# A new order for the opening of the second layer: batch 0's keys and key pieces before all queries, batch 0's probabilities inside the first substitution

## Chip, cores and metric

The kernel runs on one core of a Trainium2 chip. The metric is the device time of one execution in microseconds (us), as the median of several runs; lower is better. The engines are PE (TensorE matmuls, with PEld for its weight loads), DVE (VectorE), ACT (ScalarE), POOL (GpSimd) and SP, which issues most of the transfers.

## What is computed

Two transformer-like layers over `x` (4 batches, 256 tokens, 256 channels). Each layer has a gated recurrent branch, an attention and a feed-forward part (ternary weights in the first, eight experts with capacity in the second). The edit touches the attention of the second layer, whose values are first corrected by a triangular solve:

```python
q, k = _rope(q, k)
s = jnp.einsum('bihd,bjhd->bhij', k, k) * scale
s = jnp.where(strict, s, -jnp.inf)
m = jnp.max(s, axis=-1, keepdims=True)
e = jnp.exp(s - m)                      # 0 where not strict
p = e / denom
L = p * beta[..., None]
A = L + jnp.eye(T)
u = jax.scipy.linalg.solve_triangular(A, v, lower=True)
sc = jnp.where(causal, jnp.einsum('bihd,bjhd->bhij', q, k) * scale, -jnp.inf)
o = jnp.einsum('bhij,bhjd->bihd', softmax(sc), u) @ Wo
```

## The kernel before

The work is a list of steps, `ORDER`, that `make_order` (from line 253) writes out by hand. Every engine runs through this list and issues, for each step, the part that is its own; so the list sets the order on PE, ACT, POOL and SP. For DVE the function `lag` moves some steps a little later. Semaphores order the engines against one another; within one engine nothing overtakes.

For batch b of the second layer the steps are these.

- `requant` b (DVE L1806 to L1810) adds the quantized feed-forward output of the first layer to `x`; `gate` 2 b (ACT tanh L1329, DVE L1634) makes the layer's input.
- `proj` 1 b 1 projects the keys, `proj` 1 b 0 the queries: PE, then the rotation on DVE (L1652 to L1655). `split` cuts the result into three bfloat16 parts on DVE (L1664 to L1672). SP stores the parts to memory (L816) and loads them again in another layout, the stacks (L804): behind a key split eight loads (stack `k` and stack `kq`), behind a query split none; the four loads of stack `q` are the step `qload`. There are three `k` stacks, two `kq` and two `q`. The parts of keys, and those of queries, have one buffer each, so a split waits until the last store of its kind has landed.
- `kscores` (nine pieces): keys against keys on PE, the row maxima on DVE (L1687 to L1695), exponentials with their sums on ACT (L1408). `kmax` turns the maxima on PE (L1033) and copies them on ACT (L1364), and SP puts them as rows below the stack `kq` (L852). `kdiag` then gives the diagonal blocks transposed (PE, ACT L1385), `den` and `blocks` scale them (DVE L1825 to L1836), and POOL inverts all 32x32 blocks of the batch in a chain of small operations (L2077 to L2086). `kprobs` (eight pieces) gives the blocks below the diagonal (PE, ACT L1392).
- `inverse` b: DVE moves POOL's result out (L1845). POOL starts the next batch's blocks only behind that. Then eight rounds of `solve` (PE, DVE copy L1867, SP copies L866) and `update` (PE L1138, DVE L1853 and L1856): the substitution.
- `vproj` projects the values (PE, ACT L1354, DVE L1819). `scores` (twelve pieces, DVE maxima L1705), `minus` and `max`, `probs` (twelve pieces, ACT L1373) and `pv` are the attention with the solved values.

Most steps that write to PSUM take one of four banks in turn, the ring `mid`; PE waits until the step four places earlier in that ring has been read.

The steps of later batches are put between the rounds of the substitution by `spread`: `ahead[b]` is the list of what is done during batch b's. In the kernel before, all keys and queries of batches 0 and 1 come first, then the key pieces; the `probs` of batch 0 and the `vproj` of batch 2 stand right ahead of `inverse` 0, and the first substitution holds batch 2's key pieces, batch 3's keys, queries and values, and batch 1's scores.

Of the kernel before, what the change touches and what calls it, by code (L numbers as in the profile page):

```python
# [38 lines left out]
B, T, D = 4, 256, 256  # L39
# [26 lines left out]
NK = 3  # L66
# [188 lines left out]
def make_order():  # L255
    def groups(kind, layer, b):
        n = {"kscores": KG, "kprobs": KP}.get(kind, NGS[layer])
        return [(kind, layer, b, j) for j in range(n)]


    o = first_layer()[0]

    def vproj(b):
        return [("vproj", b, 0), ("vproj", b, 1)]
# [4 lines left out]
    def otr(b):  # L269
        return [[("otr", 1, b, 0)], [("otr", 1, b, 1)]]  # L270

    def keys_then_queries(b):
        return [("proj", 1, b, 1), ("split", 1, b, 1), ("proj", 1, b, 0), ("split", 1, b, 0)]

    o += [("requant", 0), ("gate", 2, 0)] + keys_then_queries(0) + [("qload", 0)] + vproj(0) + [("requant", 1), ("gate", 2, 1)]
    o += keys_then_queries(1) + [("qload", 1)] + vproj(1) + [("requant", 2), ("requant", 3), ("gate", 2, 2)]
    o += groups("kscores", 1, 0) + [("kmax", 1, 0)] + groups("scores", 1, 0)[:6] + [("kdiag", 0, 0), ("kdiag", 0, 1), ("den", 0), ("blocks", 0)]
    o += groups("kprobs", 1, 0) + groups("scores", 1, 0)[6:] + [("minus", 1, 0), ("max", 1, 0)]
    o += groups("kscores", 1, 1) + [("kmax", 1, 1)] + keys_then_queries(2)
    o += [("kdiag", 1, 0), ("kdiag", 1, 1), ("den", 1), ("blocks", 1)] + groups("kprobs", 1, 1) + groups("probs", 1, 0) + [("qload", 2)] + vproj(2)  # L280

    def one_each(steps):
        return [[step] for step in steps]

    def queries(b):
        return one_each(groups("scores", 1, b)) + [[("minus", 1, b), ("max", 1, b)]]

    def out(b):
        return [[("oT", 1, b)], [("wo", 1, b), ("gate", 3, b)]]

    p1, p2, p3 = (one_each(groups("probs", 1, b)) for b in range(1, B))
    def inverted(b):
        return one_each(groups("kscores", 1, b)) + [[("kmax", 1, b)]], [[("kdiag", b, 0)], [("kdiag", b, 1), ("den", b), ("blocks", b)]]

    (k2, d2), (k3, d3) = inverted(2), inverted(3)
    ahead = [k2 + [[("gate", 2, 3)], [("proj", 1, 3, 1), ("split", 1, 3, 1)]] + d2 + [[("proj", 1, 3, 0), ("split", 1, 3, 0)]] + one_each(vproj(3))
             + queries(1),
             k3 + otr(0) + d3 + p1[:4] + [[("oT", 1, 0)]] + p1[4:8] + out(0)[1:] + p1[8:] + [[("qload", 3)]] + queries(2),
             otr(1) + p2[:4] + [[("oT", 1, 1)]] + p2[4:8] + out(1)[1:] + p2[8:]
             + queries(3),  # L300
             otr(2) + p3[:4] + [[("oT", 1, 2)]] + p3[4:8] + out(2)[1:] + p3[8:]]
    for b in range(B):

# [25 lines left out]


ORDER = make_order()


# [97 lines left out]
def program(nc, d):  # L431

    with ExitStack() as ctx:
# [69 lines left out]
        oT = v3(take(CT * T), CT)  # L503
# [180 lines left out]
        ones_ready = sem("ones_rows_ready")  # L684
# [13 lines left out]
        parts_ready = [sem(f"{n}_parts_ready") for n in ("q", "k")]  # L698
# [196 lines left out]
        def _(pe):  # L895
# [14 lines left out]
            for step in ORDER:  # L910
                kind = step[0]
                i = count.get(kind, 0)
                count[kind] = i + 1
                if kind == "proj":
                    layer, b = step[1:3]
# [6 lines left out]
                    for o in step[3:] or (0, 1):  # L922
                        out = bank_of(slot) if layer else big(slot, o)
# [11 lines left out]
                elif kind == "vproj":  # L935

                    _, b, a = step
# [35 lines left out]
                elif kind == "kdiag":  # L973

                    _, b, a = step
                    pe.wait_ge(mrows["kq", b % 2], row_count("kq", 1, b))
                    if b == 0:
                        pe.wait_ge(ones_ready, NK)
                    slot = acquire(step)
                    q_, k_ = stack["kq", b % 2], stack["k", stack_of("k", 1, b)]  # L980
                    mask = maskb[:, KQ_STRICT, :]
# [1034 lines left out]
        def _(pool):  # L2016
# [19 lines left out]
            for step in ORDER:  # L2036
# [14 lines left out]
                elif kind == "quant":  # L2051
                    pool.wait_ge(amax_in, 1)
                    G_.partition_all_reduce(small[:, 65:66], small[:, 64:65], P, RED.max).then_inc(amax_out, 1)
                    pool.wait_ge(amax_out, 1)
                elif kind == "qload" and step[1] == 0:
                    pool.wait_ge(parts_ready[0], B + 1)
                    wait_done(pool, ("fc2", B - 1), "act")
                    pool.wait_ge(gate_ready, NUMBER["weigh", 3, B - 1] + 1)
                    ones_rows(2)
# [120 lines left out]
```

## Time and profile before

| | us |
|---|---|
| median of 3 runs (lowest, highest) | 781.09 (777.92, 781.1) |
| the profiled execution | 783.57 |
| its span in the trace | 781.8 |
| first layer | about 0 to 314 |
| POOL inverts batch 0's blocks | 377.43 to 420.61 |
| DVE moves the inverses of batches 0 to 3 | 424.88, 484.74, 549.45, 593.35 |

The span is the time from the first instruction of the trace to the last; the profiled execution's own time also holds what lies around it. A timeline row gives start and duration, the engine, the line of the kernel, the operation with its operands, a count, and in brackets how long the engine had been idle and what released it. Consecutive equal instructions are merged into one row with the start of the first and the time to the end of the last.

### The profile page before, as it was taken

Reading aid. Unit: us, or ns where it says so; the run is one execution under the profiler, and the core shown is the slowest. Engines: PE = TensorE matmul, PEld = TensorE weight load, DVE = VectorE, ACT = ScalarE, POOL = GpSimd, SP = SyncE. Lnnn points to the kernel's source line nnn. Section 1 sums busy time; section 2 is a strip of 40 time slices with the busy share of each in tenths; the row PEclk is TensorE's granted clock in tenths of the full one; section 3 lists DMA queues with packets and bytes.
Section 4 is the critical chain, followed back from the end, with each engine's and each line's share of the span. In section 5 each row is a group of like instructions: output and inputs, shape, how many; then the busy total and the mean of one; then the engine's idle time right before and its main releaser. Section 6 shows DMA issues by size and latency. Waiting matters only on the chain.

```text
span 781.8 us, 17527 instructions
## 1 busy us (share of the span) xinstructions
PE 512.3 (66%) x7117; PEld 416.5 (53%) x7117; DVE 566.9 (73%) x1184; ACT 329.5 (42%) x779; POOL 214.1 (27%) x313
## 2 busy tenths in 40 slices
PE   0451754895595853444647577758887873799995
PEld 0341643784485742332435355536654653799995
DVE  6899599797859994678676877666475446768861
ACT  4335243453355622006365611433411343368771
POOL 3000000000000000000685881880683001325443
PEclk9965656896798977665667676659898856699999
DMA  8055005032000020175007133002202238256622
GB/s 310 22 118 122 0 18 105 1 85 38 1 2 1 1 55 0 49 156 122 4 3 158 13 75 61 7 5 49 64 10 63 31 143 283 88 153 204 191 29 27
DMA packets 48209, 56.02 MB, mean 72 GB/s; under 512 B 25136, under 2 KB 42048, under 8 KB 43648
## 3 DMA queue, kind: packets, MB, share of 16 engines
q1 hardware_dynamic: 44784, 49.90, 24.7%
q0 software_dynamic: 3344, 4.99, 3.4%
q8 instruction: 56, 0.92, 0.5%
q14 instruction: 25, 0.20, 0.1%
HBM read 43.15 MB, written 10.49 MB: 69 GB/s over the span
## 4 chain that ended last, share of the span: by engine, by line
PE 37%; DVE 27%; issue 8%; ACT 4%; DMA 1%; POOL 1%; SPq 0%; POOLq 0%; DVEq 0%; ACTq 0%
PE psum L904 32%; DVE arena L1705 3%; PE psum L1138 3%; DVE arena L1687 2%; DVE arena L1856 2%; ACT psum L1408 1%; DVE arena L1692 1%; DVE arena L1695 1%; DVE arena L1693 1%; DVE arena L1853 1%; DVE arena L1590 1%; DVE arena L1618 1%; DVE arena L1634 1%; DVE psum L1654 1%; DVE arena L1655 1%
## 5 line engine op out<-in xcount | busy, mean ns | idle before, releaser
L904 PE MATMUL psum<-arena 32*32 32x16 f32 (+20 forms) x5281 | 354.6, 278 | 192.1 <-DVE arena L1634 76.6
L904 PEld LDWEIGHTS psum<-arena 98*32 98x32 bf16 (+8 forms) x5281 | 273.6, 128 | 269.7 <-DVE arena L1634 79.3
L2086 POOL TENSOR_TENSOR arena<-arena 128x31 f32<-128x31 f32 (+15 forms) x124 | 69.0, 556 | 9.7
L1705 DVE TENSOR_REDUCE arena<-psum 128x4 f32<-128x1024 f32 (+2 forms) x80 | 59.7, 789 | 11.6 <-PE psum L904 11.1
L1373 ACT ACTIVATE arena<-psum 128x512 f32<-128x512 f32 (+1 forms) x80 | 50.5, 687 | 40.0 <-PE psum L904 40.0
L2084 POOL TENSOR_TENSOR arena<-arena 128x31 f32<-128x31 f32 (+15 forms) x124 | 64.4, 520 | 9.7
L1408 ACT ACTIVATE psum<-psum,arena 128x256 f32<-128x256 f32 (+7 forms) x128 | 45.3, 367 | 27.8 <-DVE arena L1695 27.5
L1604 DVE TENSOR_TENSOR_SCAN arena<-arena 128x255 f32<-128x255 f32 x64 | 42.5, 727 | 11.4 <-ACT arena L1318 11.3
L2065 POOL DMA_DIRECT2D arena<-wq x1 | 0.9, 862 | 171.9 <-PE psum L904 171.9
L1318 ACT ACTIVATE arena<-arena 128x255 f32<-128x255 f32 x64 | 27.2, 498 | 46.4 <-DVE arena L1590 46.4
L2110 POOL DMA_INDIRECT out<-arena x16 | 31.2, 1948 | 48.9 <-DVE arena L2010 46.8
L2100 POOL DMA_INDIRECT arena<-dispatched,arena x16 | 19.6, 1227 | 84.7 <-DVE arena L1977 81.0
L1992 DVE TENSOR_TENSOR fc_second_parts<-arena,fc_first_parts 128x2048 fp32r<-128x2048 f32 x16 | 36.6, 2290 | 7.8 <-ACT fc_first_parts L1515 7.7
L904 PE MATMUL psum<-input_first_parts,fc_first_parts 128*128 128x256 f32 x128 | 39.0, 305 | 1.3 <-DVE input_second_parts L1986 1.3
L1487 ACT ACTIVATE psum<-psum,arena 128x256 f32<-128x256 f32 x64 | 24.6, 448 | 35.7 <-PE psum L904 35.7
L1138 PE MATMUL psum<-arena 32*32 32x224 f32 (+6 forms) x896 | 36.2, 307 | 5.0 <-DVE arena L1867 3.0
L1590 DVE TENSOR_TENSOR_SCAN arena<-arena 128x256 f32<-128x256 f32 x64 | 39.0, 672 | 0.5
L904 PE MATMUL psum<-fc_first_parts,hidden_first_parts 128*128 128x256 f32 x128 | 36.8, 288 | 2.5 <-DVE hidden_second_parts L2003 2.5
L904 PE MATMUL psum<-input_second_parts,fc_first_parts 128*128 128x256 f32 x128 | 38.2, 299 | 0.0
L904 PE MATMUL psum<-input_first_parts,fc_second_parts 128*128 128x256 f32 x128 | 38.2, 298 | 0.0
L904 PE MATMUL psum<-fc_first_parts,hidden_second_parts 128*128 128x256 f32 x128 | 36.2, 283 | 0.0
L904 PE MATMUL psum<-fc_second_parts,hidden_first_parts 128*128 128x256 f32 x128 | 36.2, 283 | 0.0
(185 smaller groups left out, 890.4 us busy)
## 6 DMA issues: line engine op xcount, KB each, us to landing
arena<-fc SPq DMA_DIRECT2D x16, 1024.0 KB, 5.0
arena<-parts SPq DMA_DIRECT2D x40, 256.0 KB, 4.6
parts<-arena SPq DMA_DIRECT2D x16, 384.0 KB, 3.6
arena<-parts SPq DMA_DIRECT2D x40, 128.0 KB, 5.5
arena<-arena SPq DMA_DIRECT2D x128, 8.0 KB
arena<-xT SPq DMA_DIRECT2D x1, 1024.0 KB, 10.4
arena<-w1T SPq DMA_DIRECT2D x1, 1024.0 KB, 10.8
arena<-w2T SPq DMA_DIRECT2D x1, 1024.0 KB, 13.0
```

Source lines behind the costliest of these rows:

```text
L904: return nc.tensor.matmul(out, lhsT, rhs, start=start, stop=stop)
L1138: last = nc.tensor.matmul(acc(half)[rows, qq, (s + 1) * BLK:T], ublk[rows, s, q, :], later[b % 2][s][rows, q, :], start=s == 0 and qq == 0 ...
L1318: A(scan[s + 1][:, ct, 0:T - 1], scan[s][:, ct, 0:T - 1], ACT.Copy, scale=back[:, i:i + 1]).then_inc(scaled, 1)
L1373: ins = A(prob[:, first:end, 0:T] if early else prob[:, first:end, T:T + P], src, ACT.Exp, scale=scale)
L1408: ins = A(s_, s_, ACT.Exp, bias=nbias[:, n:n + 1], accum_out=ncc[b][:, n:n + 1])
L1590: ins = V.tensor_tensor_scan(scan[s][:, ct, :], dd, src[:, ct, bt(b)], 0.0, ALU.mult, ALU.add)
L1604: st(V.tensor_tensor_scan(scan[s][:, ct, T - 2::-1], dd, scan[s + 1][:, ct, T - 2::-1], scan[s][:, ct, T - 1:T], ALU.mult, ALU.add))
L1705: ins = V.tensor_reduce(mneg[:, at + first:at + end], src, axis=AX.X, op=ALU.max, negate=True)
L1992: V.tensor_tensor(second[:], fcw[e % NW][i], first[:].bitcast(F32), ALU.subtract).then_inc(w_second[i], 1)
L2084: link(G_.tensor_tensor(tmp, A3[:, k + 1:BLK, k:k + 1].to_broadcast([P, rows, w]), X3[:, k:k + 1, 0:w].to_broadcast([P, rows, w]), ALU.mult))
L2086: ins = G_.tensor_tensor(X3[:, k + 1:BLK, 0:w], X3[:, k + 1:BLK, 0:w], tmp, ALU.add)
L2110: G_.indirect_dma_start(out=d["out"], out_offset=bass.IndirectOffsetOnAxis(ap=ids[:, 2 * e + s:2 * e + s + 1], axis=0), in_=eo[e % 2][:, s ...
```

## The change

Only the order changes, with two waits that follow from it.

- Keys and queries are separate steps now. Batch 0's keys and its `vproj` come first, then the remaining three `requant`, the second `gate`, and batch 0's key pieces at once. Batch 1's keys follow, then the inverse's blocks of batch 0, and only then the queries of batches 0 and 1.
- Batch 1's key pieces stand behind that; batch 0's scores and batch 1's blocks behind those; batch 2's keys last.
- Batch 2's queries and `vproj` and batch 0's `probs` move into the first substitution. The `probs` alternate with batch 2's key pieces; batch 2's queries stand right ahead of batch 3's.
- POOL clears the third stack's rows of ones and the padding of the solution behind batch 0's key split instead of behind its `qload`. The `kdiag` of batches 0 and 2 wait for the rows of ones of their own stack.

```diff
-    def keys_then_queries(b):
-        return [("proj", 1, b, 1), ("split", 1, b, 1), ("proj", 1, b, 0), ("split", 1, b, 0)]
-
-    o += [("requant", 0), ("gate", 2, 0)] + keys_then_queries(0) + [("qload", 0)] + vproj(0) + [("requant", 1), ("gate", 2, 1)]
-    o += keys_then_queries(1) + [("qload", 1)] + vproj(1) + [("requant", 2), ("requant", 3), ("gate", 2, 2)]
-    o += groups("kscores", 1, 0) + [("kmax", 1, 0)] + groups("scores", 1, 0)[:6] + [("kdiag", 0, 0), ("kdiag", 0, 1), ("den", 0), ("blocks", 0)]
-    o += groups("kprobs", 1, 0) + groups("scores", 1, 0)[6:] + [("minus", 1, 0), ("max", 1, 0)]
-    o += groups("kscores", 1, 1) + [("kmax", 1, 1)] + keys_then_queries(2)
-    o += [("kdiag", 1, 0), ("kdiag", 1, 1), ("den", 1), ("blocks", 1)] + groups("kprobs", 1, 1) + groups("probs", 1, 0) + [("qload", 2)] + vproj(2)
+    def keys(b):
+        return [("proj", 1, b, 1), ("split", 1, b, 1)]
+
+    def queries_of(b):
+        return [("proj", 1, b, 0), ("split", 1, b, 0)]
+
+    o += [("requant", 0), ("gate", 2, 0)] + keys(0) + vproj(0) + [("requant", 1), ("requant", 2), ("requant", 3), ("gate", 2, 1)]
+    o += groups("kscores", 1, 0) + [("kmax", 1, 0)] + keys(1) + [("kdiag", 0, 0), ("kdiag", 0, 1), ("den", 0), ("blocks", 0)]
+    o += queries_of(0) + [("qload", 0)] + groups("kprobs", 1, 0) + queries_of(1) + [("qload", 1)] + vproj(1)
+    o += groups("kscores", 1, 1) + [("kmax", 1, 1), ("gate", 2, 2)] + groups("scores", 1, 0)[:6]
+    o += [("kdiag", 1, 0), ("kdiag", 1, 1), ("den", 1), ("blocks", 1)] + groups("scores", 1, 0)[6:] + [("minus", 1, 0), ("max", 1, 0)]
+    o += keys(2) + groups("kprobs", 1, 1)
...
-    ahead = [k2 + [[("gate", 2, 3)], [("proj", 1, 3, 1), ("split", 1, 3, 1)]] + d2 + [[("proj", 1, 3, 0), ("split", 1, 3, 0)]] + one_each(vproj(3))
-             + queries(1),
+    p0 = one_each(groups("probs", 1, 0))
+    mixed = [unit for pair in zip(k2, p0) for unit in pair] + p0[len(k2):]
+    ahead = [mixed + one_each(vproj(2)) + [[("gate", 2, 3)], keys(3)] + d2 + [queries_of(2), [("qload", 2)], queries_of(3)]
+             + one_each(vproj(3)) + queries(1),
...
-                    if b == 0:
-                        pe.wait_ge(ones_ready, NK)
+                    if b in (0, NK - 1):
+                        pe.wait_ge(ones_ready, b + 1)
...
-                elif kind == "qload" and step[1] == 0:
-                    pool.wait_ge(parts_ready[0], B + 1)
+                elif step == ("split", 1, 0, 1):
+                    pool.wait_ge(parts_ready[1], B + 1)
```

The lines of the changed kernel are four higher behind the edit (L1687 is L1691 there, and so on).

The first place is on DVE, behind the last key piece of batch 0. Before, batch 0's scores (L1705) followed, then `den` and `blocks`:

```order
L1687 TENSOR_REDUCE arena<-psum 128x4
L1692 TENSOR_SCALAR arena<-arena 128x4
L1693 SCALAR_TENSOR_TENSOR arena<-arena 128x4
L1695 TENSOR_TENSOR arena<-arena 128x4
L1705 TENSOR_REDUCE arena<-psum 128x2 x2
L1705 TENSOR_REDUCE arena<-psum 128x4
L1705 TENSOR_REDUCE arena<-psum 128x2 x2
L1705 TENSOR_REDUCE arena<-psum 128x4
L1825 TENSOR_SCALAR arena<-arena 128x32
```

Now the rotation (L1656 to L1659) and the split (L1668 to L1676) of batch 1's keys follow, then `den`:

```order
L1691 TENSOR_REDUCE arena<-psum 128x4
L1696 TENSOR_SCALAR arena<-arena 128x4
L1697 SCALAR_TENSOR_TENSOR arena<-arena 128x4
L1699 TENSOR_TENSOR arena<-arena 128x4
L1656 TENSOR_TENSOR arena<-psum,arena 128x512
L1658 TENSOR_TENSOR psum<-psum,arena 128x512
L1659 TENSOR_TENSOR arena<-arena,psum 128x512
L1668 CAST arena<-arena 128x512
L1673 TENSOR_TENSOR arena<-arena 128x512
L1674 CAST arena<-arena 128x512
L1676 TENSOR_TENSOR arena<-arena 128x512
L1829 TENSOR_SCALAR arena<-arena 128x32
```

What followed DVE's own pieces were scores, whose matmuls PE could do ahead; now it is a projection that PE issues behind `kmax`.

The second place is on DVE around the move of batch 0's inverse (L1845, now L1849), which the first `solve` copy and the first key piece of batch 2 follow. Before, `blocks` of batch 1 and the `vproj` of batch 2 (L1819) stood ahead of it, and batch 2's keys had been split earlier:

```order
L1836 STREAM_TRANSPOSE arena<-arena 128x1024
L1819 TENSOR_TENSOR arena<-psum,arena 128x16 x2
L1845 STREAM_TRANSPOSE arena<-arena 128x32x32
L1867 COPY arena<-psum 128x2x16 x2
L1687 TENSOR_REDUCE arena<-psum 128x2
```

Now the rotation and split of batch 2's keys stand right ahead of it:

```order
L1656 TENSOR_TENSOR arena<-psum,arena 128x512
L1658 TENSOR_TENSOR psum<-psum,arena 128x512
L1659 TENSOR_TENSOR arena<-arena,psum 128x512
L1668 CAST arena<-arena 128x512
L1673 TENSOR_TENSOR arena<-arena 128x512
L1674 CAST arena<-arena 128x512
L1676 TENSOR_TENSOR arena<-arena 128x512
L1849 STREAM_TRANSPOSE arena<-arena 128x32x32
L1871 COPY arena<-psum 128x2x16 x2
L1691 TENSOR_REDUCE arena<-psum 128x2
```

Between the split of batch 2's keys and the first piece that uses them, DVE now has the move and one `solve` copy.

The third place is on SP, in the first substitution from batch 3's key store on. L816 stores parts, L804 loads stacks, L866 copies the solution. Before, one query store stood behind the eight loads:

```order
L816 DMA parts<-arena 128x6x256
L804 DMA arena<-parts 32x4096 x2
L804 DMA arena<-parts 16x4096 x3
L804 DMA arena<-parts 32x4096 x2
L804 DMA arena<-parts 16x4096
L866 DMA arena<-arena 32x4x16 x4
L816 DMA parts<-arena 128x6x256
L866 DMA arena<-arena 32x4x16 x16
```

Now batch 2's query store and its four loads come behind the key loads, and batch 3's query store behind them (the lines are L820, L808 and L870):

```order
L820 DMA parts<-arena 128x6x256
L808 DMA arena<-parts 32x4096 x2
L808 DMA arena<-parts 16x4096 x3
L808 DMA arena<-parts 32x4096 x2
L808 DMA arena<-parts 16x4096
L820 DMA parts<-arena 128x6x256
L808 DMA arena<-parts 16x4096
L808 DMA arena<-parts 32x4096 x2
L808 DMA arena<-parts 16x4096
L870 DMA arena<-arena 32x4x16 x4
L820 DMA parts<-arena 128x6x256
L870 DMA arena<-arena 32x4x16 x8
```

Two query stores, with a set of loads between them, stand where one stood.

## Rows read from the trace of the kernel before

**Rows 1.** The page: the span, and each engine's busy time.
```profile
span 781.8 us, 17527 instructions
PE 512.3 (66%) x7117; PEld 416.5 (53%) x7117; DVE 566.9 (73%) x1184; ACT 329.5 (42%) x779; POOL 214.1 (27%) x313
```
**Rows 2.** Timeline of POOL: batch 0's inverse starts and ends, batch 1's starts.
```profile
377.43 1.91 POOL L2077 TENSOR_TENSOR arena<-arena 128x1024 f32<-128x1024 f32 x1 [43.48 <-DVEq L1838]
...
420.36 0.25 POOL L2086 TENSOR_TENSOR arena<-arena 128x31 f32<-128x31 f32 x1
426.96 1.91 POOL L2077 TENSOR_TENSOR arena<-arena 128x1024 f32<-128x1024 f32 x1 [6.35 <-DVE arena L1845]
```
**Rows 3.** Timeline of DVE: batch 2's vproj, and the moves of the four inverses.
```profile
424.67 0.17 DVE L1819 TENSOR_TENSOR arena<-psum,arena 128x16 f32<-128x16 f32 x1 [0.77 <-ACT arena L1354]
424.88 1.91 DVE L1845 STREAM_TRANSPOSE arena<-arena 128x1024 f32<-128x1024 f32 x1
...
484.74 1.99 DVE L1845 STREAM_TRANSPOSE arena<-arena 128x1024 f32<-128x1024 f32 x1
...
549.45 1.97 DVE L1845 STREAM_TRANSPOSE arena<-arena 128x1024 f32<-128x1024 f32 x1
...
593.35 1.97 DVE L1845 STREAM_TRANSPOSE arena<-arena 128x1024 f32<-128x1024 f32 x1 [3.69 <-POOL arena L2086]
```
**Rows 4.** Timeline of SP: batch 0's key store, key loads, query store, query loads.
```profile
326.34 0.39 SPq L816 DMA_DIRECT2D parts<-arena  x1
329.11 3.56 SPq L804 DMA_DIRECT2D arena<-parts  x8
332.70 0.42 SPq L816 DMA_DIRECT2D parts<-arena  x1
341.08 1.70 SPq L804 DMA_DIRECT2D arena<-parts  x4
```
**Rows 5.** Timeline of DVE: batch 0's keys, a requant, first and last key piece.
```profile
321.79 0.69 DVE L1652 TENSOR_TENSOR arena<-psum,arena 128x512 f32<-128x512 f32 x1 [3.94 <-PE psum L904]
...
331.32 1.74 DVE L1806 TENSOR_SCALAR arena<-arena 128x512 f32<-128x512 f32 x1
...
354.94 0.69 DVE L1687 TENSOR_REDUCE arena<-psum 128x2 f32<-128x512 f32 x1
...
366.21 0.17 DVE L1695 TENSOR_TENSOR arena<-arena 128x4 f32<-128x4 bf16 x1
```
**Rows 6.** Timeline of PE: the diagonal blocks of batch 0.
```profile
372.70 2.69 PE L904 MATMUL psum<-arena 98*32 98x32 bf16 x154 [1.72 <-DMA arena<-arena]
```
**Rows 7.** Timeline of DVE: batch 1's key pieces, batch 2's keys and first piece.
```profile
385.37 0.69 DVE L1687 TENSOR_REDUCE arena<-psum 128x2 f32<-128x512 f32 x1 [1.02 <-PE psum L904]
...
400.87 0.57 DVE L1695 TENSOR_TENSOR arena<-arena 128x4 f32<-128x4 bf16 x1
405.27 0.69 DVE L1652 TENSOR_TENSOR arena<-psum,arena 128x512 f32<-128x512 f32 x1 [3.83 <-PE psum L904]
...
409.99 0.99 DVE L1672 TENSOR_TENSOR arena<-arena 128x512 bf16<-128x512 f32 x1
...
427.83 0.69 DVE L1687 TENSOR_REDUCE arena<-psum 128x2 f32<-128x512 f32 x1 [0.17 <-PE psum L904]
```
**Rows 8.** Groups by line, DVE, 317 to 485: score reductions (busy, mean ns, idle).
```profile
L1705 DVE TENSOR_REDUCE arena<-psum 128x2 f32<-128x512 f32 (+1 forms) x24 | 15.5, 687 | 3.9 <-PE psum L904 3.8
```
**Rows 9.** Windows: stretch, length, busy PE, PEld, DVE, ACT, POOL; PE clock; DMA.
```profile
427.30:447.40 20.10, 11.44 (x352) 7.61 (x344) 16.47 (x60) 12.65 (x66) 17.69 (x31) 0.70 0.24 41
427.30:484.74 57.44, 38.66 (x976) 26.24 (x964) 46.05 (x137) 15.22 (x70) 38.34 (x65) 0.69 0.31 60
560.00:580.00 20.00, 18.44 (x381) 13.06 (x381) 12.43 (x48) 7.73 (x14) 17.81 (x29) 0.91 0.10 11
```
**Rows 10.** Timeline of DVE: first solve copy behind batch 3's key projection.
```profile
454.50 0.34 DVE L1867 COPY arena<-psum 128x32 f32<-128x32 f32 x2 [4.31 <-PE psum L904]
```
**Rows 11.** Timeline of ACT: the twelve probs of batch 0.
```profile
417.12 6.23 ACT L1373 ACTIVATE arena<-psum 128x512 f32<-128x512 f32 x12
```

More of the change, by code:

```diff
@@ L295, in make_order @@
     (k2, d2), (k3, d3) = inverted(2), inverted(3)
-    ahead = [k2 + [[("gate", 2, 3)], [("proj", 1, 3, 1), ("split", 1, 3, 1)]] + d2 + [[("proj", 1, 3, 0), ("split", 1, 3, 0)]] + one_each(vproj(3))
-             + queries(1),
+    p0 = one_each(groups("probs", 1, 0))
+    mixed = [unit for pair in zip(k2, p0) for unit in pair] + p0[len(k2):]
+    ahead = [mixed + one_each(vproj(2)) + [[("gate", 2, 3)], keys(3)] + d2 + [queries_of(2), [("qload", 2)], queries_of(3)]
+             + one_each(vproj(3)) + queries(1),
              k3 + otr(0) + d3 + p1[:4] + [[("oT", 1, 0)]] + p1[4:8] + out(0)[1:] + p1[8:] + [[("qload", 3)]] + queries(2),
-             otr(1) + p2[:4] + [[("oT", 1, 1)]] + p2[4:8] + out(1)[1:] + p2[8:]
-             + queries(3),
+             otr(1) + p2[:4] + [[("oT", 1, 1)]] + p2[4:8] + out(1)[1:] + p2[8:] + queries(3),
              otr(2) + p3[:4] + [[("oT", 1, 2)]] + p3[4:8] + out(2)[1:] + p3[8:]]
```

## The prediction

> **What bounds the kernel now.** I read the page's totals first [rows 1]: no engine is busy throughout (DVE 73%, PE 66%), so the time is a chain of hand-overs and has to be read stage by stage. The edit touches one stage, from the end of the first layer (about 314 us) to the inverse of batch 1. The timelines of POOL and DVE mark it. POOL inverts batch 0's diagonal blocks from 377.43 to 420.61, 43.2 us, and starts batch 1's only at 426.96, when DVE has moved the first result out [rows 2]. DVE moves it at 424.88, 4.3 us after POOL was done: it had first to finish with the last `vproj` of batch 2, whose second half it took at 424.67 [rows 3]. So the first substitution starts late because PE, ACT and DVE still had work queued ahead of it, and not because of POOL. It ends where DVE moves batch 1's inverse, 484.74, and the next at 549.45. The third wait is 3.69 us for POOL [rows 3], and POOL cannot start that inverse before 549.45. Everything behind 484.74 is in the same order in both kernels and hangs on that move, with no slack that could swallow a delay or a lead. I therefore price one number: **when DVE moves the inverse of batch 1**, 484.74 now.
>
> **The opening, walked with the rows.** No instruction is added or removed on PE, DVE, ACT or POOL; all the cost is in waits. Up to the split of batch 0's keys nothing changes (its store leaves SP at 326.34). Its eight key loads are issued from 329.11; the query store behind them, issued 332.70, is seen landed at 341.08 [rows 4]. In the new order this store is later, so the loads alone have to land: between 338 (a fifth less data) and 341; I take 339.0, 12.7 us after the split. Until then DVE does the first `vproj`, all three remaining requants and the second gate: about 10 us even if the first requant is slowed by POOL's clearing as now (1.74 us for the first of its instructions [rows 5]). They cost nothing; their cover is this wait.
>
> Batch 0's k pieces start on DVE at 339.2 instead of 354.94, and take 11.4 us as now, to 350.6 [rows 5]. From there the maxima take 6.3 us to reach PE's `kdiag` (366.38 to 372.70 [rows 5, 6]), so 356.9. In between DVE has to wait for the key projection of batch 1, which PE may start only when DVE has ended the pieces: such a wait was 3.94 us [rows 5] and 3.83 us [rows 7]. Then 4.5 us of rotation and split (321.79 to 326.31), to 358.9, and 3 us for `den` and `blocks`. POOL starts at about 362, **15 us earlier**, and is done with batch 0 at 405.
>
> DVE is not. It still has: the queries of batches 0 and 1 (4.5 us each, 5.7 while POOL runs, as from 405.27 to 410.98 [rows 7]; waits for PE of 1 and 3 us between, by estimate), to 377.5; the k pieces of batch 1, 16.1 us under POOL (385.37 to 401.44 [rows 7]), to 393.5; an estimated 3 us until the gate, which then stands behind the last maxima copy on ACT; twelve score reductions of 0.69 us [rows 8] and some 4 us for `den`, `blocks` and `minus`, to 409; a wait of 3.8 for PE's projection of batch 2's keys and 4.5 us of rotation and split. That split ends at about **417** (410.98 now), and DVE moves inverse 0 right behind it, at 417 instead of 424.88. So far the change is ahead by 8 us.
>
> **Where I think the lead goes.** The substitution cannot use it. Behind the first `solve`, PE has the first k piece of batch 2, which needs the loads of the keys just split: 417 plus the same 12.7 us is 429.7, while now this split is 17 us old when DVE takes the piece (410.98 to 427.83 [rows 7]). That piece comes at about 429.8 then: **+2.0**, bounds -8 (waits of the walk that overlap, solve at once) and +6 (two waits more). These terms come on top, inside the substitution:
>
> - Batch 2's query rotation and split and its `vproj` move behind that point. 4.5 us plus 0.4, **+5.0**. Cover: DVE is idle for 11.4 of the 57.4 us there (46.05 busy [rows 9]), but these are waits for PE, such as 4.31 us for batch 3's projection [rows 10], that stay. Bounds 0 and 5.7.
> - A new wait: batch 3's query split follows batch 2's at once, and the buffer of its pieces is free only when batch 2's query store has landed. SP issues that store behind batch 3's eight key loads. A store behind eight loads took 8.4 us (332.70 to 341.08), one alone 2.8 (326.34 to 329.11) [rows 4]. Key split at Y: loads landed Y+12.3, store Y+14.8, DVE at the second split Y+11.7. **+3.0**, bounds 0 and 3.5. SP's copies of the solution stand behind the query loads too; they have until the end of the substitution.
> - Batch 0's twelve `probs` now stand one by one between k pieces, which share four PSUM banks with them. ACT took 6.2 us for twelve [rows 11] and is busy for 12.65 of the 20.1 us in which batch 2's pieces run; PE for 11.44 [rows 9]. Both have room for the nine that fall there, barely; the last three and `vproj` stand on PE ahead of the update and of the solve that DVE waits for, 3 us of waits, of which some are there now. **+2.5**, bounds 0 and +6.
> - DVE idles during some 10 us of POOL's second inverse, so less of its work is slowed (5.7 against 4.5 us per split): **-1.5**, bounds -2.5 and 0.
>
> Sum: 2.0 + 5.0 + 3.0 + 2.5 - 1.5 = **+11.0 us**. The profiled execution took 783.57 us (span 781.8 and 1.8 around it), so 794.6. It is 2.5 above the median of the three runs, 781.09, and I forecast for the median: **792.0 us**. As a check: the second substitution, which already holds a batch's pieces, `probs` and scores, takes 64.7 us (484.74 to 549.45 [rows 3]); the first would be at some 78 us with three projections more and 9 us of waiting for the loads.
>
> **TensorE's clock** speaks against my sum. In the stretch of batch 2's pieces PE was busy 11.4 of 20.1 us at a granted 0.70, the mean of a stretch between its two levels, 1.2 and 2.4 GHz; in a stretch where it was busy 18.4 of 20 us it was 0.91 [rows 9]. With `probs` among the pieces PE works more, so the clock may stay up, and DVE's waits for PE shorten: the 4.31 [rows 10] by up to half, the other short ones likewise; all the idle time there is 11.4, so I take 5 us at the most. My sum takes none of it, since the same stretch begins with PE standing still for 9 us. The Trainium skill ("TensorE: Matmul & The Clock Gate", Part 1) states that the clock is throttled by default and that activity releases it; by that rule the denser order gains and the sum would be 787 instead of 792; the two rows go its way, but in neither does PE first stand still.
>
> **Rivals.**
> - *The lead is kept* (chance 0.19). If the three waits of 3 to 4 us that I gave DVE for PE's projections overlap with other work, the split ends near 407, the loads are there at 420, and DVE takes the first piece 7.8 us earlier; if the added work also fits into the 11.4 idle us, the kernel takes 773. For it: POOL's head start of 15 us is real in the walk. It decides at a split before 408. Against: the same wait of 3.8 us shows now wherever a projection follows pieces.
> - *It evens out* (0.15). The added terms vanish in DVE's idle time and only the 2.0 of the first piece stays: 783.
> - *The clock stays up* (0.14): 11.0 less 5 gives 787.
> - *A jam* (0.12). The banks shared with `probs`, PE in order and SP's queue each at the upper bound: 2 + 5.7 + 3.5 + 6, and 1 in the opening, gives 799.
> - The rest, 0.40, is the forecast. That the change does not do what it says is no rival: the order of the instructions shows the moves.
>
> **How the numbers follow.** Half a percent, 3.9 us, is about what a measurement of this kernel can tell from no change; the three runs lie 0.4% apart. The forecast, the clock case and the jam are slower by more: 0.40 + 0.14 + 0.12 = 0.66. The even case gives 0.15 for no change, the kept lead 0.19 for faster. The range goes from 777, which takes in the even case and half of a kept lead, to 799, the jam: about 0.15 is left out.
>
> **What would show it.** Right: POOL's first inverse starts near 362; DVE's first k piece of batch 2 comes 10 us or more after the move of inverse 0, released by PE that waited for a DMA; batch 3's query split waits for a store; the move of inverse 1 is near 496. Wrong: that first piece comes within 3 us of the move of inverse 0, or the move of inverse 1 lies before 485. A higher granted clock between the two moves, with the update waits shortened, would speak for the clock.

## The result, and the profile after

The changed kernel takes 799.08 us (median of 4 runs, 796.33 to 800.86) against 779.77 (4 runs): a ratio of 1.0242, interval 1.0209 to 1.0275. It is slower. In e3 below one run of six was disturbed, and its median is that of the other five. The changed kernel's profiled execution took 796.33 us with a span of 794.5. The busy times on the page are those of [rows 1] within 1% on every engine but PE's weight loads (2.4%), so the 19 us are waits:

```profile
span 794.5 us, 17528 instructions
PE 507.9 (64%) x7117; PEld 406.3 (51%) x7117; DVE 567.1 (71%) x1184; ACT 328.8 (41%) x779; POOL 212.3 (27%) x313
```

The first layer happened to end 1.5 us earlier in this profile, so stages are compared from the first requant. Its row on DVE's timeline, before the change:

```profile
314.26 0.49 DVE L1806 TENSOR_SCALAR arena<-arena 128x512 f32<-128x512 f32 x1
```

DVE's timeline of the changed kernel: the first requant, the first key piece of batch 0, the split of batch 2's keys, the move of inverse 0 and the first solve copy, the first key piece of batch 2, batch 3's query split, the move of inverse 1. Between them stand two waits of the opening: 4.18 us for batch 1's key projection, and 2.14 us in the split of batch 1's queries.

```profile
312.79 0.48 DVE L1810 TENSOR_SCALAR arena<-arena 128x512 f32<-128x512 f32 x1
...
339.15 0.69 DVE L1691 TENSOR_REDUCE arena<-psum 128x2 f32<-128x512 f32 x1 [4.88 <-PE psum L908]
...
354.75 0.69 DVE L1656 TENSOR_TENSOR arena<-psum,arena 128x512 f32<-128x512 f32 x1 [4.18 <-PE psum L908]
...
374.26 0.81 DVE L1668 CAST arena<-arena 128x512 bf16<-128x512 f32 x1 [2.14 <-DMA parts<-arena]
...
417.33 0.69 DVE L1676 TENSOR_TENSOR arena<-arena 128x512 bf16<-128x512 f32 x1
418.06 1.91 DVE L1849 STREAM_TRANSPOSE arena<-arena 128x1024 f32<-128x1024 f32 x1
420.57 0.34 DVE L1871 COPY arena<-psum 128x32 f32<-128x32 f32 x2 [0.60 <-PE psum L908]
432.46 0.69 DVE L1691 TENSOR_REDUCE arena<-psum 128x2 f32<-128x512 f32 x1 [11.55 <-PE psum L908]
...
490.80 0.43 DVE L1668 CAST arena<-arena 128x512 bf16<-128x512 f32 x1 [4.30 <-DMA parts<-arena]
...
504.12 1.96 DVE L1849 STREAM_TRANSPOSE arena<-arena 128x1024 f32<-128x1024 f32 x1
```

POOL's timeline: it starts batch 0's inverse at 362.30, ends it at 405.78, and then stands idle until DVE has moved the result.

```profile
362.30 1.91 POOL L2081 TENSOR_TENSOR arena<-arena 128x1024 f32<-128x1024 f32 x1 [34.38 <-DVEq L1842]
...
405.53 0.25 POOL L2090 TENSOR_TENSOR arena<-arena 128x31 f32<-128x31 f32 x1
420.14 1.91 POOL L2081 TENSOR_TENSOR arena<-arena 128x1024 f32<-128x1024 f32 x1 [14.36 <-DVE arena L1849]
```

The first inverse starts 13.7 us earlier than in [rows 2], counted from the requant, and its result is moved 5.4 us earlier than in [rows 3]. DVE had the longer queue. The first key piece of batch 2 is nevertheless **6.1 us later**, and its 11.55 us of idleness are PE's, which waits for the loads of the keys split at 418.02:

```profile
431.74 2.02 PE L908 MATMUL psum<-arena 96*32 96x256 bf16 x27 [11.09 <-DMA arena<-parts]
```

SP's timeline shows the other wait. Batch 2's query store (484.35) follows batch 3's eight key loads. Its own loads, which wait for it to land, go out at 490.72. DVE's split of batch 3's queries resumes at 490.80. The wait of 2.14 us in the opening is of the same kind, batch 1's queries behind batch 0's store; the kernel before has none there.

```profile
475.40 0.38 SPq L820 DMA_DIRECT2D parts<-arena  x1
478.79 3.55 SPq L808 DMA_DIRECT2D arena<-parts  x8
484.35 0.38 SPq L820 DMA_DIRECT2D parts<-arena  x1
490.72 1.69 SPq L808 DMA_DIRECT2D arena<-parts  x4
```

From that first piece to the move of inverse 1, windows of both kernels (stretch, length, busy PE, PEld, DVE, ACT, POOL; PE clock, DMA share, GB/s), before:

```profile
427.83:484.74 56.91, 38.13 (x949) 25.76 (x937) 45.69 (x135) 15.22 (x70) 37.81 (x65) 0.69 0.30 58
```

and after, with the stretch between the move of inverse 0 and the first piece ahead of it:

```profile
418.06:432.46 14.40, 1.35 (x45) 0.94 (x46) 2.24 (x3) 0.72 (x3) 10.80 (x19) 0.50 0.72 139
432.46:504.12 71.66, 47.69 (x1129) 30.38 (x1128) 51.16 (x144) 21.64 (x84) 25.68 (x46) 0.75 0.28 55
```

The stretch is **14.75 us** longer: 5.5 are DVE's added work (batch 2's queries and `vproj`), 9.3 are added idleness of DVE (20.5 against 11.2). Together, 6.1 and 14.75, the move of inverse 1 comes 20.9 us later. The second substitution is then 3.5 us shorter (61.19 against 64.71).

Most of that lies at its start, between the move of inverse 1 and the first solve copy, where PE has the same 213 matmuls to do. Before:

```profile
484.74:494.55 9.81, 8.65 (x213) 6.65 (x217) 1.99 (x2) 4.51 (x14) 6.74 (x11) 0.55 0.05 8
```

and after:

```profile
504.12:511.37 7.25, 7.00 (x213) 5.47 (x217) 1.97 (x3) 4.55 (x14) 4.67 (x6) 0.76 0.03 6
```

That is 2.6 us less: 1.65 of it is PE's busy time at a granted clock of 0.76 in place of 0.55, the rest PE's idle time.

### The profile page after: what moved, and what is told of

The parts are those of the page before. It is cut to its first block, busy times and chain, and to the rows that moved or that the text cites. A ratio compares the mean times of both kernels' runs of the same rounds, so it can differ in the third digit from the quotient of the medians.

```text
span 794.5 us, 17528 instructions
## 1 busy us (share of the span) xinstructions
PE 507.9 (64%) x7117; PEld 406.3 (51%) x7117; DVE 567.1 (71%) x1184; ACT 328.8 (41%) x779; POOL 212.3 (27%) x313
## 4 chain that ended last, share of the span: by engine, by line
PE 33%; DVE 25%; issue 8%; DMA 5%; ACT 5%; SPq 1%; POOL 1%; POOLq 0%; DVEq 0%; ACTq 0%
PE psum L908 29%; DVE arena L1709 3%; PE psum L1142 3%; DVE arena L1860 2%; DMA parts<-arena 2%; DVE arena L1691 2%; ACT psum L1412 2%; DMA arena<-parts 2%; DVE arena L1696 1%; DVE arena L1697 1%; DVE arena L1857 1%; DVE arena L1699 1%; DVE arena L1594 1%; DVE arena L1622 1%; DVE arena L1673 1%
## 5 line engine op out<-in xcount | busy, mean ns | idle before, releaser
L908 PE MATMUL psum<-arena 32*32 32x16 f32 (+23 forms) x5281 | 350.6, 274 | 215.5 <-DVE arena L1638 65.3
L908 PEld LDWEIGHTS psum<-arena 98*32 98x32 bf16 (+8 forms) x5281 | 265.5, 126 | 296.8 <-DVE arena L1638 67.1
L2090 POOL TENSOR_TENSOR arena<-arena 128x31 f32<-128x31 f32 (+15 forms) x124 | 67.4, 544 | 9.7
L2088 POOL TENSOR_TENSOR arena<-arena 128x31 f32<-128x31 f32 (+15 forms) x124 | 64.2, 517 | 9.7
L1142 PE MATMUL psum<-arena 32*32 32x224 f32 (+6 forms) x896 | 38.5, 316 | 1.3 <-issue 1.2
L1691 DVE TENSOR_REDUCE arena<-psum 128x2 f32<-128x512 f32 (+7 forms) x60 | 26.1, 466 | 17.3 <-PE psum L908 17.1
L2081 POOL TENSOR_TENSOR arena<-arena 128x1024 f32<-128x1024 f32 x4 | 7.6, 1908 | 111.9 <-DVE arena L1849 77.5
```

Of the source, the lines that this page charges most:

```text
L908: return nc.tensor.matmul(out, lhsT, rhs, start=start, stop=stop)
L1142: last = nc.tensor.matmul(acc(half)[rows, qq, (s + 1) * BLK:T], ublk[rows, s, q, :], later[b % 2][s][rows, q, :], start=s == 0 and qq == 0 ...
L1691: st(V.tensor_reduce(mneg[:, s, qs], score_cols(slot, g, s), axis=AX.X, op=ALU.max, negate=True))
L2088: link(G_.tensor_tensor(tmp, A3[:, k + 1:BLK, k:k + 1].to_broadcast([P, rows, w]), X3[:, k:k + 1, 0:w].to_broadcast([P, rows, w]), ALU.mult))
L2090: ins = G_.tensor_tensor(X3[:, k + 1:BLK, 0:w], X3[:, k + 1:BLK, 0:w], tmp, ALU.add)
```

## The experiments

The theory: three separate costs. The loads of keys split too late (A), probabilities in the first substitution (B), the query split that waits for a store behind eight loads (C). The rival in each case is that the cost is hidden anyway, by one of the others or by POOL. Each of the first three runs undoes one part of the change, the fourth all three.

**e1, probabilities ahead again (B).**

```diff
-    o += keys(2) + groups("kprobs", 1, 1)
+    o += keys(2) + groups("kprobs", 1, 1) + groups("probs", 1, 0)
...
-    mixed = [unit for pair in zip(k2, p0) for unit in pair] + p0[len(k2):]
+    mixed = k2
```

> The changed kernel with one part undone: batch 0's twelve probs stand ahead of the move of inverse 0 again, behind batch 1's kprobs; all else as changed. My theory: PE does them in the 11.5 us in which it waits for batch 2's key loads, and they no longer stand between the key pieces, so the stretch from the first key piece of batch 2 to the end of batch 3's key split (42.9 us in the changed kernel, 32.6 before) shrinks to about 35, the first piece stays at 432, and the kernel takes about 791, 8 below the changed one. Rival (the stretch is long because of the values and the later rounds of the substitution in it, not because of the probs): the stretch stays above 41 and the time within 2 us of 799.

Measured 795.4 us, ratio 1.0158 (1.0112 to 1.0204), 4 us above the forecast. The first piece stayed and the stretch to the move of inverse 1 shrank by 5.2 us, so the theory held in direction.

**e2, batch 2's keys earlier (A).**

```diff
-    o += groups("kscores", 1, 1) + [("kmax", 1, 1), ("gate", 2, 2)] + groups("scores", 1, 0)[:6]
+    o += groups("kscores", 1, 1) + [("kmax", 1, 1), ("gate", 2, 2)] + keys(2) + groups("scores", 1, 0)[:6]
...
-    o += keys(2) + groups("kprobs", 1, 1)
+    o += groups("kprobs", 1, 1)
```

> The changed kernel with batch 2's keys moved up, behind the gate of batch 2 and ahead of batch 0's scores; all else as changed. My theory: their loads (about 13 us from the split) are landed when the substitution starts, so the 11.55 us in which DVE waits ahead of the first key piece vanish; that piece comes 2 to 4 us after the move of inverse 0, which stays near 418, and the kernel takes about 789, 10 below the changed one. Rival (the substitution is held by the inverse of batch 1 on POOL or by the shared banks, so an earlier start is waited away again): below 3 us.

Measured 788.51 us, ratio 1.0078 (1.0051 to 1.0106), as forecast.

**e3, batch 2's queries ahead of batch 3's keys (C).**

```diff
-    ahead = [mixed + one_each(vproj(2)) + [[("gate", 2, 3)], keys(3)] + d2 + [queries_of(2), [("qload", 2)], queries_of(3)]
+    ahead = [mixed + one_each(vproj(2)) + [queries_of(2), [("qload", 2)], [("gate", 2, 3)], keys(3)] + d2 + [queries_of(3)]
```

> The changed kernel with batch 2's queries ahead of batch 3's keys instead of right ahead of batch 3's queries, so that their store is landed when batch 3's queries are split. My theory: the 4.3 us in which DVE waits for a store there vanish and nothing takes their place: about 795, 4 below the changed one. Rival (a wait for PE or for the scores' loads takes its place): within 1.5 us of 799.

Measured 793.6 us, ratio 1.0109 (1.0068 to 1.0149). That is 5.5 us below the changed kernel by the medians and 10 by the ratios; in the stage it is 6.0 at the move of inverse 1.

**e4, all three.** Its edit is those of e1 to e3 together.

> The three edits together: batch 2's keys early, batch 0's probs ahead of inverse 0, batch 2's queries apart from batch 3's. My theory: 10 less for the loads, 8 less for the probs in the stretch, 4 less for the store, but some 7 us of probs now delay the first solve since no wait for loads covers them: about 784, still some 4 above the kernel before. Rival (POOL's head start of 15 us counts once the waits are gone): 775 or less.

Measured 782.98 us, ratio 1.0027 (1.0001 to 1.0053), as forecast.

In e2 the first piece follows the first solve copy at once, as DVE's timeline shows; the 11.55 us are gone:

```profile
421.92 0.34 DVE L1871 COPY arena<-psum 128x32 f32<-128x32 f32 x2 [2.12 <-PE psum L908]
422.65 0.69 DVE L1691 TENSOR_REDUCE arena<-psum 128x2 f32<-128x512 f32 x1 [0.39 <-PE psum L908]
```

Windows from the first piece of batch 2 to the move of inverse 1 (columns as above), of e1:

```profile
434.02:500.52 66.50, 39.00 (x1085) 27.00 (x1077) 50.73 (x145) 15.87 (x72) 26.48 (x47) 0.76 0.29 59
```

of e2:

```profile
422.65:494.10 71.45, 47.97 (x1129) 30.73 (x1128) 51.84 (x145) 21.83 (x85) 34.39 (x64) 0.75 0.28 56
```

of e3:

```profile
433.38:500.13 66.75, 49.28 (x1129) 32.47 (x1128) 50.69 (x144) 21.65 (x84) 26.23 (x47) 0.70 0.30 59
```

and of e4:

```profile
428.30:490.30 62.00, 39.05 (x1085) 27.98 (x1073) 49.99 (x145) 16.35 (x74) 30.12 (x53) 0.77 0.32 64
```

DVE's idle time in the stretch (length less busy) is 20.5 in the changed kernel, 15.8 in e1, 19.6 in e2, 16.1 in e3, 12.0 in e4, 11.2 before. Thus B costs 4.7 and C 4.4, and undoing both with A as well, in e4, gives 8.5: neither hid the other. The stretch to batch 3's key split that I had also named for e1 came out at 35.2 against 42.9, as expected, but it overstates B, since the shorter list puts that split one round of the solve earlier.

A and B do not add up. Two marks from each profile, the first piece of batch 2 (counted from the first requant) and the move of inverse 1 (counted from that piece), in us:

| | first piece | to the move of inverse 1 | sum |
|---|---|---|---|
| before | 113.6 | 56.9 | 170.5 |
| changed | 119.7 | 71.7 | 191.3 |
| e1 | 119.7 | 66.5 | 186.2 |
| e2 | 109.5 | 71.5 | 181.0 |
| e3 | 118.6 | 66.8 | 185.3 |
| e4 | 115.2 | 62.0 | 177.2 |
| e7 | 113.0 | 70.8 | 183.8 |
| e5 | 104.6 | 61.9 | 166.5 |
| e6 | 107.5 | 61.7 | 169.2 |
| e8 | 106.2 | 58.4 | 164.6 |
| e9 | 98.7 | 61.6 | 160.3 |

Probabilities ahead of the inverse cost nothing in e1, where PE waits for the loads anyway, and 5.7 us in e4 (115.2 against 109.5 in e2), where it does not: the first solve waits 8.21 us for PE there, which has batch 1's `kprobs` and the probabilities to do first.

```profile
427.89 0.29 DVE L1870 COPY arena<-psum 128x32 f32<-128x32 f32 x2 [8.21 <-PE psum L907]
```

So without all three costs the new order is still no better than the old one. Its opening also holds DVE's waits of 4.18 and 3.94 us for single projections and 2.29 for a gate. The next experiments ask whether the head start of the early keys can be used at all.

**e7, the changed kernel with its opening closed up alone.**

```diff
-    o += [("requant", 0), ("gate", 2, 0)] + keys(0) + vproj(0) + [("requant", 1), ("requant", 2), ("requant", 3), ("gate", 2, 1)]
-    o += groups("kscores", 1, 0) + [("kmax", 1, 0)] + keys(1) + [("kdiag", 0, 0), ("kdiag", 0, 1), ("den", 0), ("blocks", 0)]
-    o += queries_of(0) + [("qload", 0)] + groups("kprobs", 1, 0) + queries_of(1) + [("qload", 1)] + vproj(1)
+    o += [("requant", 0), ("gate", 2, 0)] + keys(0) + vproj(0) + [("requant", 1), ("gate", 2, 1), ("requant", 2), ("requant", 3)] + keys(1)
+    o += groups("kscores", 1, 0) + [("kmax", 1, 0)] + queries_of(0) + [("qload", 0), ("kdiag", 0, 0), ("kdiag", 0, 1), ("den", 0), ("blocks", 0)]
+    o += queries_of(1) + [("qload", 1)] + groups("kprobs", 1, 0) + vproj(1)
```

> The changed kernel with its opening closed up and nothing else: batch 1's keys ahead of batch 0's key pieces, batch 0's queries between the turning of its maxima and its diagonal blocks, batch 1's queries ahead of batch 0's kprobs. Batch 2's keys, the probabilities and the queries in the substitution stay as the change has them. Theory: the waits of the opening (4.2 us for the projection, and 4.5 us of split that now fit under the wait for the loads) are on the path; the move of inverse 0 comes 8 us earlier, near 410, all behind it by as much, and the kernel takes 791 us against 799. Rival: POOL's inverse, ending near 405, or the gate takes the lead back; then 796 or more.

Measured 794.93 us, ratio 1.0197 (1.0149 to 1.0245). The move of inverse 0 comes 6.6 us earlier than in the changed kernel (8 expected), that of inverse 1 7.6; the ratios lie only 0.0045 apart, and their intervals overlap. In the stage the theory held; how much of it reaches the end is not settled by these runs.

**e5, e4 with that opening**, both next gates in it, and batch 2's key projection among batch 1's pieces:

```diff
-    o += groups("kscores", 1, 1) + [("kmax", 1, 1), ("gate", 2, 2)] + keys(2) + groups("scores", 1, 0)[:6]
+    o += groups("kscores", 1, 1)[:5] + [("proj", 1, 2, 1)] + groups("kscores", 1, 1)[5:] + [("kmax", 1, 1), ("split", 1, 2, 1)] + groups("scores", 1, 0)[:6]
```

> The kernel of e4, with the opening closed up as well: batch 1's keys and both next gates stand ahead of batch 0's key pieces (DVE idles 5.2 us there for the loads), batch 0's queries stand between the turning of its maxima and its diagonal blocks (a wait of some 6 us), and batch 2's key projection stands among batch 1's pieces. If the opening is bound by DVE's waits for single PE projections (4.2, 3.9 and 2.3 us in e4), DVE reaches the move of inverse 0 when POOL is done with it, near 406 instead of 417.7, the first piece of batch 2 comes near 411 instead of 428.3, and the kernel takes 767 us (range 764 to 773). Rival, POOL or PE take over at once: POOL's second inverse or batch 0's probabilities, which PE still does ahead of the first solve, hold the first piece at 420 or later; then 775 or more.

Measured 775.92 us, ratio 0.9953 (0.9928 to 0.9977): 0.5% faster than before, but 9 us short of the forecast. DVE moves inverse 0 at 407.92, nearly where expected. From there the rival holds: the first solve waits for PE, and the first piece comes at 418.56, not 411.

```profile
407.92 1.97 DVE L1848 STREAM_TRANSPOSE arena<-arena 128x1024 f32<-128x1024 f32 x1
418.15 0.29 DVE L1870 COPY arena<-psum 128x32 f32<-128x32 f32 x2 [8.26 <-PE psum L907]
418.56 0.69 DVE L1690 TENSOR_REDUCE arena<-psum 128x2 f32<-128x512 f32 x1
```

**e6, e5 with batch 0's probabilities ahead of batch 1's `kprobs`.**

```diff
-    o += [("kdiag", 1, 0), ("kdiag", 1, 1), ("den", 1), ("blocks", 1)] + groups("scores", 1, 0)[6:] + [("minus", 1, 0), ("max", 1, 0)]
-    o += groups("kprobs", 1, 1) + groups("probs", 1, 0)
+    o += [("kdiag", 1, 0), ("kdiag", 1, 1), ("den", 1), ("blocks", 1)]
+    o += groups("probs", 1, 0) + groups("kprobs", 1, 1)
```

(its `scores`, `minus` and `max` of batch 0 stand ahead of these lines.)

> As e5, but all of batch 0's scores with their maxima stand ahead of batch 1's diagonal blocks, and its probabilities ahead of batch 1's kprobs, so that PE and ACT do them while DVE still scales blocks. Theory: in e5 the first solve waits some 3 us for PE; here it does not, and the kernel is 2 to 3 us faster than e5, 764. Rival: the first solve waits for POOL or for batch 2's loads, and the time is that of e5 within 1 us.

Measured 779.67 us, ratio 0.9983 (0.9947 to 1.0018). It missed both ways: 3.8 us above e5 in the median (the intervals overlap a little), with a new wait on PE's timeline, for the copy of the row of maxima that the probabilities need:

```profile
410.25 11.38 PE L907 MATMUL psum<-arena 98*128 98x256 bf16 x212 [3.64 <-DMA arena<-arena]
```

In e5 the `kprobs` cover that copy.

**e8, e5 with batch 1's `kprobs` in two halves behind its diagonal blocks and behind batch 0's scores**, and the last gate in the opening:

```diff
-    o += [("kdiag", 1, 0), ("kdiag", 1, 1), ("den", 1), ("blocks", 1)] + groups("scores", 1, 0)[6:] + [("minus", 1, 0), ("max", 1, 0)]
-    o += groups("kprobs", 1, 1) + groups("probs", 1, 0)
+    o += [("kdiag", 1, 0), ("kdiag", 1, 1)] + groups("kprobs", 1, 1)[:4] + [("den", 1), ("blocks", 1)] + groups("scores", 1, 0)[6:] + groups("kprobs", 1, 1)[4:] + [("minus", 1, 0), ("max", 1, 0)]
+    o += groups("probs", 1, 0)
```

> The kernel of e5 with two more moves. Batch 1's kprobs go, in two halves, behind its diagonal blocks and behind batch 0's scores, where PE idles some 4 us in e5 (402.4 to 404.3, 406.0 to 408.1); the last gate of the opening goes ahead of batch 0's key pieces (in the substitution PE waits 4.5 us for it). Theory: the first solve of e5 waits 8.3 us for PE because kprobs and probabilities, 10.5 us, stand ahead of it in one block; with 4 us of it gone the wait is 4 to 5 us, the gate gives 1 to 2 more, and the kernel takes 771 us (768 to 773). Rival: DVE's scores then wait for banks that kprobs hold, the move of inverse 0 comes later by what was gained, and the time is that of e5, 776, within 2 us.

Measured 773.95 us, ratio 0.9912 (0.9881 to 0.9944), 1 us above the forecast range. The wait of the first solve did not shrink: 9.12 us, and PE itself waits 2.62 us in it for the same copy.

```profile
417.85 0.29 DVE L1870 COPY arena<-psum 128x32 f32<-128x32 f32 x2 [9.12 <-PE psum L907]
```

What it gains over e5 comes later (58.4 us in the stretch against 61.9), though the intervals of the two overlap.

**e9, e8 with the probabilities in the substitution, behind the pieces.**

```diff
-    o += groups("probs", 1, 0)
...
-    ahead = [mixed + one_each(vproj(2)) + [queries_of(2), [("qload", 2)], keys(3)] + d2 + [queries_of(3)]
+    ahead = [mixed + one_each(groups("probs", 1, 0)) + one_each(vproj(2)) + [queries_of(2), [("qload", 2)], keys(3)] + d2 + [queries_of(3)]
```

> As e8, but batch 0's twelve probabilities stand in the first substitution again, behind the last key piece of batch 2 in place of among the pieces. Theory of the shared banks: what costs time in the change is that the probabilities alternate with the pieces in the same four banks; behind the pieces, where PE idles 6.9 us, most of them are free, the first solve follows the move of inverse 0 at once (the first piece near 411) and the kernel takes 768 us. Rival: the probabilities cost the substitution PE and ACT time wherever they stand; the stretch from the first piece to batch 3's key split grows from 32 to 39 us or more, and the kernel takes 772 us or more, no better than e8.

Measured **770.6 us**, ratio 0.9847 (0.9803 to 0.9892), 1.5% faster than the kernel before. It lies 3.4 us below e8, though their intervals overlap a little, and 2.6 above the forecast. Its rows on DVE, the move of inverse 0, the first solve copy and the first piece (the first requant is at 314.86 here):

```profile
410.36 1.90 DVE L1847 STREAM_TRANSPOSE arena<-arena 128x1024 f32<-128x1024 f32 x1
412.87 0.34 DVE L1869 COPY arena<-psum 128x32 f32<-128x32 f32 x2 [0.60 <-PE psum L906]
413.60 0.69 DVE L1689 TENSOR_REDUCE arena<-psum 128x2 f32<-128x512 f32 x1 [0.40 <-PE psum L906]
```

Windows of the stretch, of e9 and then of e8:

```profile
413.60:475.16 61.56, 44.83 (x1129) 30.72 (x1121) 49.44 (x143) 21.98 (x83) 36.70 (x65) 0.76 0.33 64
```

```profile
418.26:476.69 58.43, 40.85 (x1085) 29.12 (x1073) 49.06 (x144) 15.64 (x72) 29.14 (x51) 0.72 0.32 67
```

The first piece comes 7.5 us earlier than in e8, counted from the requant, and the probabilities give 3.1 of it back in the stretch. The stretch that the expectation names, 32 us there, is the one to the first split, which is that of batch 2's queries; it grows from 32.6 to 36.7, so the rival holds in part. POOL ends its first inverse at 407.73, 406.79 and 409.53 in e5, e8 and e9, and DVE moves the result 0.2, 0.04 and 0.8 us later: there DVE no longer lets the result wait.

## Why the forecast was right in sign and 7 us short

- **What bounds the stage.** Right. The head start of POOL arrived (13.7 us, forecast 15), but only 5.4 us of it reached the move of inverse 0 (forecast 8), because DVE was not done. The *kept lead* needed a split before 408; it ended at 418.02, which is 419.5 counted as before the change.
- **First key piece of batch 2, +2.0.** It was +6.1, at the upper bound of 6. Two parts were mis-sized: the split came 2.5 us later than my 417, and the first piece came 14.4 us behind it where I took 12.7: PE's first matmul on the loads started after 13.7, and its piece had to be done. I had read the 12.7 as a discount on the 14.8 us that a set of loads and a store took in [rows 4, 5]. Batch 0's own loads had none of that size either: from the split, which ended at 324.84, to the first piece at 339.15, 14.3 us. That piece was forecast for 339.2 and came at 340.6 counted as before, so 1.4 of the 2.5 are the same error, made a first time at the start of the opening. There the wait for a query store, 2.14 us, was not named; its time was inside the 4 us that I allowed for PE. e2 shows what the wait is worth: with the keys earlier, the first piece comes 10.1 us sooner, and the time falls from 1.0242 to 1.0078 of before.
- **Batch 2's queries and `vproj`, +5.0**, and **POOL relief, -1.5.** DVE's busy time in the stretch rose by 5.5: the work was priced right, a net relief did not show.
- **The query split's wait for the store, +3.0.** The wait is there, at the instruction named: 4.30 us, and 4.4 less idleness when e3 takes it away. It lies above my bound of 3.5. e3 does not touch the same wait in the opening.
- **Probabilities among the pieces, +2.5.** Measured 4.7 in e1, within the bounds of 0 and 6. Their place matters: in length of the stretch they cost 5.2 among the pieces (71.7 against 66.5) and 3.1 behind them (e9 against e8), in two orders that differ in other steps too. PE's waits in the stretch for ACT's exponentials of the pieces, which hold a bank until they are done, come to 6.0 us with the probabilities among the pieces and 3.4 in e1, and to 3.8 behind them against 2.2 in e8. So a part of the cost shows there; that the banks shared with the pieces make the difference was argued, not shown by itself.
- **The clock.** It did rise, from 0.69 to 0.75 in the stretch, between the levels of 1.2 and 2.4 GHz, and stood at 0.50 while PE waited for the loads (418.06 to 432.46, busy 1.35 of 14.4 us). In the stretch it bought nothing that could be seen: DVE's idle time rose by 9.3 us. The rule of the Trainium skill ("TensorE: Matmul & The Clock Gate", Part 1), that activity releases the throttle, agrees with that low stretch; the 5 us that I worked out by it did not come. e3, with PE busier than in the changed kernel (49.3 of 66.8 us against 47.7 of 71.7), was granted less, 0.70.
- **Everything behind the move of inverse 1** I took as unchanged. The second substitution is 3.5 us shorter; it is 61.0 to 63.8 in the profiles of all the experiments, too. Here the clock counts: the 213 matmuls ahead of the first solve copy keep PE busy for 6.9 to 8.7 us in the eleven profiles, longest before the change, where the granted clock is lowest (0.55). Why it is lower there was not tried; PE had been busy for 5.5 of the 8 us ahead of the move before and 5.4 after, at 0.71 and 0.83. So 20.9 us at the move of inverse 1 are 17.3 at the next; the medians differ by 19.3, and single profiles scatter by a few us (that of before was 3.8 above its median, that of after 2.8 below).

The sum of +11.0 was 20.9 at the move of inverse 1: counted as before the change, DVE did it at 505.6 and not near 496. Of the 9.9 missing, 4.1 were in the first piece and 5.8 in the stretch: there 2.2 for the probabilities, 1.4 for the store wait, and 2.0 for the queries with the relief that did not show. The result is that of the *jam* (799, chance 0.12) by size, but only in part by its cause. All terms came out above their middle value: the first piece and the store wait lie just above their upper bounds, the probabilities within theirs. The jam's 18.2 has 3 us for the opening and the first piece, where 6.1 were measured, and meets 20.9 at that move, of which 3.5 came back behind it. That the time is the jam's 799 is therefore luck. What was measured lies 7 us above the forecast of 792.

## What to carry to other kernels

Starting the longest unit earlier helps only if the engine that picks up its result is free by then: count that engine's queue to the hand-over before moving anything, here DVE's waits of 4 us for one projection at a time. Where a step's data pass through memory, the split's store and its loads are one latency, 14 us here, to be covered with other work on both sides; moving the split next to its use puts all of it on the path. And what is moved out of a block may have been covering something: `kprobs` hid the copy of the maxima that the probabilities wait for.

## What the runs showed that I had not expected

Where DVE waits for the loads, the first piece comes nearly the same time behind the end of the key split: 14.3 and 14.4 us in the changed kernel, 14.2 in e1, 13.9 in e3 and 14.3 in e7. PE's row for batch 0's first piece in the changed kernel:

```profile
338.35 2.22 PE L908 MATMUL psum<-arena 96*32 96x256 bf16 x72 [15.54 <-DMA arena<-parts]
```

No store follows these loads. Before the change one did, and had landed after 14.8 (326.31 to 341.08); when the loads ahead of it had landed, no row shows. And a block of work ahead of a solve was worth nothing or 5.7 us, by whether PE waited for loads behind it: e1 and e4 hold the same twelve probabilities at the same place.
